# A recurrent loop on one core: side products ahead of the LSTM's, h's rest written twice, one unread product fewer per joint step

## What is computed

```python
x = x + delta_rule(lstm(x, cond), ...)      # L2_cond, L2_attn
x = x + bit_ffn(rnn(x, cond), ...)          # L2_cond2, L2_ffn

def lstm_step(h, c, xz_t):
    i, f, o, g = split(xz_t + h @ Wh)
    c = sigmoid(f) * c + sigmoid(i) * tanh(g)
    h = sigmoid(o) * tanh(c)

def delta_step(S, k, v, q, beta):           # 8 heads of 32 x 32 for each of 8 sequences
    kn = k / (norm(k) + 1e-6)
    delta = v - S @ kn
    S = tanh(beta[..., None] * S + delta[..., None] * kn[..., None, :])
    out = (S @ q) * silu(S @ q)

def rnn_step(h, xw_t):
    h = tanh(h @ Wh + xw_t)
```

## Time and profile before

| | us |
|---|---|
| median of 3 runs | 3003.81 |
| lowest and highest run | 2982.01, 3019.12 |
| the profiled execution | 3002.12 |
| its span | 3000.3 |
| busy: PE, PEld, DVE, ACT, POOL | 2498.8, 1771.7, 1727.2, 1106.1, 749.5 |

### The profile page before, as it was taken

One profiled execution on the slowest core, in us unless ns is written; L12 is line 12 of the kernel. 1 busy time (PEld: TensorE's weight loads), 2 busy tenths in 40 slices (PEclk: granted clock), 3 DMA queues, 4 the chain that ended last, 5 costly groups with the idle time before them and its releaser, 6 DMA issues. The chain is left out here.

```text
span 3000.3 us, 92538 instructions
## 1 busy us (share of the span) xinstructions
PE 2498.8 (83%) x37349; PEld 1771.7 (59%) x37354; DVE 1727.2 (58%) x7330; ACT 1106.1 (37%) x3986; POOL 749.5 (25%) x1227
## 2 busy tenths in 40 slices
PE   5998888882898889778898888889956878999998
PEld 3556666662555566555666666665533556777774
DVE  3554555556354544347776777775443865666674
ACT  1332333332133223234545555554444433333332
POOL 2210000000220000126666675766533310000000
PEclk9996555555799779899989999997856975899899
DMA  2000000001000000134645646463310000000000
GB/s 88 3 2 2 2 2 2 2 2 39 2 3 2 0 1 0 66 68 77 119 79 89 115 84 121 77 123 75 67 42 1 2 2 2 2 3 2 2 2 15
DMA packets 223769, 103.97 MB, mean 35 GB/s; under 512 B 89472, under 2 KB 220544, under 8 KB 222464
## 3 DMA queue, kind: packets, MB, share of 16 engines
q1 hardware_dynamic: 223360, 98.23, 15.9%
HBM read 89.81 MB, written 8.39 MB: 33 GB/s over the span
## 5 line engine op out<-in xcount | busy, mean ns | idle before, releaser
L649 POOL TENSOR_TENSOR l2r_beta_s<-l2r_state,l2r_beta_f 128x256 f32<-128x256 f32 x512 | 365.6, 735 | 297.7 <-ACT l2r_state L556 231.7
L556 ACT ACTIVATE l2r_state<-l2r_pre 128x256 f32<-128x256 f32 x512 | 192.7, 417 | 244.6 <-DVE l2r_pre L808 242.6
L808 DVE TENSOR_TENSOR l2r_pre<-l2r_o_ps,l2r_beta_s 128x256 f32<-128x256 f32 x512 | 194.1, 419 | 53.1 <-PE l2r_o_ps L441 32.7
L140 PE MATMUL l0r_bank<-main_x,l0r_wx_half 128*128 128x32 f32 (+2 forms) x480 | 150.1, 413 | 60.4 <-ACT l0r_out_gate L196 59.9
L140 PEld LDWEIGHTS l0r_bank<-main_x,l0r_wx_half 128*128 128x128 f32 x480 | 118.9, 311 | 81.6 <-ACT l0r_out_gate L196 79.5
L1797 PEld LDWEIGHTS l3r_bank<-main_x,l3r_wx_half 128*128 128x128 f32 x480 | 97.8, 230 | 92.6 <-issue 48.8
L441 PE MATMUL l2r_o_ps<-l2r_rows,l2r_outer 32*128 32x128 f32 x2048 | 135.1, 335 | 4.3 <-DVE l2r_rows L800 3.9
L194 ACT ACTIVATE l0r_gates<-l0r_bank 128x24 f32<-128x24 f32 x256 | 48.6, 190 | 236.3 <-PE l0r_bank L152 236.3
L1936 ACT ACTIVATE l3r_gates<-l3r_bank 128x24 f32<-128x24 f32 x256 | 48.6, 190 | 231.1 <-PE l3r_bank L1809 231.0
L228 DVE SCALAR_TENSOR_TENSOR l0r_both<-l0r_gates 128x16 f32<-128x16 f32 x256 | 45.3, 177 | 151.7 <-ACT l0r_gates L194 151.7
L152 PE MATMUL l0r_bank<-l0r_h_ring,l0r_w_part 128*128 128x8 bf16 x2304 | 102.4, 170 | 35.8 <-DVE l0r_h_ring L238 28.0
(11 more groups left out here) (590 smaller groups left out, 7324.8 us busy)
## 6 DMA issues: line engine op xcount, KB each, us to landing
l2r_beta_f<-l2r_beta_store SPq DMA_DIRECT2D x256, 256.0 KB, 7.4
main_odd_layers<-in_l SPq DMA_DIRECT2D x1, 4826.5 KB, 14.3
main_odd_layers<-in_l SPq DMA_DIRECT2D x1, 3672.0 KB, 16.2
l2r_v_store<-l2r_v_part SPq DMA_DIRECT2D x32, 96.0 KB, 3.5
l2r_v_rows<-l2r_v_store SPq DMA_DIRECT2D x16, 192.0 KB, 3.3
main_decay<-in_decay SPq DMA_DIRECT2D x1, 3072.0 KB, 10.1
main_even_layers<-in_l SPq DMA_DIRECT2D x1, 2762.5 KB, 9.6
l2r_beta_store<-l2r_beta_tok SPq DMA_DIRECT2D x64, 32.0 KB, 2.0
```

Of the source, the lines that this page charges most:

```text
L140: nc.tensor.matmul(into, wx_half[:, g * P:(g + 1) * P], x_b[:, :, w * LW + lo:w * LW + hi].rearrange("p b t -> p t b"), start=False, stop= ...
L556: nc.scalar.activation(state[:, h * 2 * P:(h + 1) * 2 * P], pre[:, h * 2 * P:(h + 1) * 2 * P], ACT.Tanh).then_inc(state_ready[h], 1)
L649: nc.gpsimd.tensor_tensor(beta_s[:, half].rearrange("p (c i) -> p c i", i=N2), state[:, half].rearrange("p (c i) -> p c i", i=N2), beta_f[ ...
L808: nc.vector.tensor_tensor(pre[:, half].rearrange("p (c n) -> p c n", c=2), o_ps[:, 2 * h:2 * h + 2, 0:P], beta_s[:, half].rearrange("p (c ...
```

## The change

Four edits, all in `recurrent_stages`:
- `UNREAD` of a joint step goes from 1 to 0; the unread product into `o_ps` stays, and so do those of the other bodies.
- TensorE's order: `lstm_pieces` (except in steps 0 and 8), `project` and `output` move from behind `lstm_products` to ahead of it, behind `spread_delta`. Their waits move with them. In steps 0 and 8 `lstm_pieces` comes ahead of the RNN's inputs.
- `split_h` has no copy any more. It writes the rest twice, into PSUM as before and with the same operands into `h_rest` in SBUF; `h_low` is the PSUM rest minus the upper half of `h_rest`, and waits for both.
- `lstm_products` reads the upper half of `h_rest` in all steps; `h_mid`, its memset and its semaphore are gone.

```diff
--- before.py
+++ after.py
@@ -255,7 +255,7 @@
 TCH = TC // 2
 SQ_STEPS = (0, 1, 2, 3, 4, 6, 7, 9)
 WIDE = 7 * B
-UNREAD = {(True, False): 2, (True, True): 1, (False, True): 3, (False, False): 0}
+UNREAD = {(True, False): 2, (True, True): 0, (False, True): 3, (False, False): 0}
 
 
 def recurrent_stages(nc, tag, x, y, wx, wh, bias, w_in, w_tok, w_q, beta_bias, w_out, sel_v, mask_r, mask_k, mask_q, mask_l, gate_sel,
@@ -271,7 +271,7 @@
         mem = Memory(nc, stack, tag)
         cand_cell, tanh_c = mem.sb("cand_cell", [P, 2 * B]), mem.sb("tanh_c", [P, B])
         h_ring = mem.sb("h_ring", [P, SLOTS, WIDE])
-        h_rest, h_mid, h_low = mem.sb("h_rest", [P, WIDE]), mem.sb("h_mid", [P, WIDE], BF16), mem.sb("h_low", [P, WIDE], BF16)
+        h_rest, h_low = mem.sb("h_rest", [P, WIDE]), mem.sb("h_low", [P, WIDE], BF16)
         w_part = [mem.sb(f"w_part{n}", [P, 4 * P], BF16) for n in range(3)]
         w_rest = mem.sb("w_rest", [P, 4 * P])
         bias_rest, bias_part = mem.sb("bias_rest", [P, 4]), mem.sb("bias_part", [P, 3, 4], BF16)
@@ -306,7 +306,7 @@
         y_b, x_b = y.rearrange("p (b t) -> p b t", t=T), x.rearrange("p (b t) -> p b t", t=T)
         x_by_half = x.rearrange("p (h b t) -> p h t b", h=2, t=T)
         names = ("consts_ready", "w_split", "bias_split", "bias_psum", "bias_ready", "xw_psum", "gates_psum", "gates_ready", "mul_ready",
-                 "cell_ready", "tanh_ready", "h_ready", "rest_ready", "h_psum", "rest_psum", "mid_h_ready", "low_ready", "xin_psum", "xp_sig_ready", "xp_ready",
+                 "cell_ready", "tanh_ready", "h_ready", "rest_ready", "h_psum", "rest_psum", "low_ready", "xin_psum", "xp_sig_ready", "xp_ready",
                  "k_psum", "v_psum", "beta_psum", "q_psum", "kv_ready", "beta_in", "q_ready", "k_sq_ready", "ssq_ready", "root_ready", "norm_ready", "inv_ready",
                  "kn_ready", "kn_stored", "kn_loaded", "v_stored", "beta_done", "beta_stored", "top_ready", "v_rested", "mid_ready",
                  "v_split", "v_loaded", "knt_psum", "knt_ready", "kn_spread", "q_spread", "outer_ready", "d_psum", "row_ready",
@@ -381,7 +381,7 @@
                     alone = n <= IN_BANK
                     if not alone:
                         pe.wait_ge(s["low_ready"], n + 1)
-                    h_parts = high(h_ring[:, (n - 1) % SLOTS, :]), high(h_rest[:, :]) if alone else h_mid[:, :], h_low[:, :]
+                    h_parts = high(h_ring[:, (n - 1) % SLOTS, :]), high(h_rest[:, :]), h_low[:, :]
                     for m in range(3):
                         if alone:
                             pe.wait_ge(s[("h_ready", "rest_ready", "low_ready")[m]], n + 1)
@@ -518,22 +518,24 @@
                         if delta is not None:
                             unread(o_ps[:, 0, :])
                             spread_delta(n)
+                        if lstm is not None and step % TCH:
+                            lstm_pieces(lstm, step, rnn)
+                        if proj is not None:
+                            project(proj, step)
+                        if out is not None:
+                            output(out, step)
                         if lstm is not None:
                             if rnn is not None and step in (0, TCH):
                                 pe.wait_ge(s["r_ready"], rnn * TC + step + 2)
                             lstm_products(lstm * TC + step)
                         if step % TCH == 0 and has_bias(k, int(step == 0)):
                             lstm_bias(*((k, 1) if step == 0 else (k + 1, 0)))
+                        if lstm is not None and step % TCH == 0:
+                            lstm_pieces(lstm, step, rnn)
                         if rnn is not None and step == 0:
                             rnn_inputs(rnn, 1, TCH + 1)
                         if rnn is not None and step == TCH:
                             rnn_inputs(rnn, TCH + 1, TC)
-                        if lstm is not None:
-                            lstm_pieces(lstm, step, rnn)
-                        if proj is not None:
-                            project(proj, step)
-                        if out is not None:
-                            output(out, step)
                         for _ in range(UNREAD[lstm is not None, delta is not None]):
                             unread(d_ps)
                         if delta is not None and n + 1 < T:
@@ -739,7 +741,6 @@
                 nc.gpsimd.tensor_tensor(w_part[2][:, :], w_rest[:, :], w_part[1][:, :], ALU.subtract).then_inc(s["w_split"], 1)
                 nc.gpsimd.memset(h_ring[:, :, B:WIDE], 0.0)
                 nc.gpsimd.memset(h_rest[:, B:WIDE], 0.0)
-                nc.gpsimd.memset(h_mid[:, B:WIDE], 0.0)
                 nc.gpsimd.memset(h_low[:, B:WIDE], 0.0)
                 nc.gpsimd.memset(kn_rows[:, :, :], 0.0)
                 nc.gpsimd.memset(v_rows[:, :, :, :], 0.0)
@@ -788,10 +789,11 @@
                     dve.wait_ge(s["h_psum"], count)
                     nc.vector.tensor_tensor(rest, lstm_at(n, 3, 4), high(h_ring[:, n % SLOTS, 0:B]),
                                             ALU.subtract).then_inc(s["rest_psum"], 1)
+                    nc.vector.tensor_tensor(h_rest[:, 0:B], lstm_at(n, 3, 4), high(h_ring[:, n % SLOTS, 0:B]),
+                                            ALU.subtract).then_inc(s["rest_ready"], 1)
                     dve.wait_ge(s["rest_psum"], count)
-                    nc.vector.tensor_copy(h_mid[:, 0:B], high(rest)).then_inc(s["mid_h_ready"], 1)
-                    dve.wait_ge(s["mid_h_ready"], count)
-                    nc.vector.tensor_tensor(h_low[:, 0:B], rest, h_mid[:, 0:B], ALU.subtract).then_inc(s["low_ready"], 1)
+                    dve.wait_ge(s["rest_ready"], n + 2)
+                    nc.vector.tensor_tensor(h_low[:, 0:B], rest, high(h_rest[:, 0:B]), ALU.subtract).then_inc(s["low_ready"], 1)
 
                 def masked(n):
                     dve.wait_ge(s["d_psum"], n + 1)
```

## The result

The changed kernel takes 3036.29 us in the median of 20 runs (2996.06 to 3066.97); the kernel before, beside it, 2998.40 in the median of 20 (2982.01 to 3021.66). So the change makes the kernel slower, by 1.3% between the medians. The ratio is only 1.0062, 95% interval [1.0034, 1.0091], because it leaves out 8 of the changed kernel's 20 runs, those over 1.5% above its fastest, and here it is the lower clock that makes runs long. Forecast were 2992 and 2958 to 3035: the median lies just above the range. The profiled execution took 3043.68 (span 3041.9, against 3000.3), with a mean granted clock of 0.791 against 0.818.

A forecast was written before the change was run, and what follows sets the result against it. It took the VectorE and ScalarE loop to bound light joint steps and beta's DMA to bound body starts. 3002.1 - 22.6 gained + 10.5 lost to the clock = 2990.0; the median, 1.7 above the profiled execution, 2992, range 2958 to 3035.

The forecast's parts named there:

- Loop (a): VectorE and ScalarE loop of a light joint step, through state, gates and h: from 2.93 to 2.80 us.
- light steps at 2.80: Joint steps with few side products on TensorE were to take 2.80 us each, as most steps would.
- h's rest: `split_h` on VectorE without the copy, L789 to the last subtraction: gain 0.12 us a step, 0.05 to 0.15.
- The unread product and the order: TensorE: 224 unread products of 0.26 us go, and side products of up to 0.55 us become free.
- loop (b): TensorE's loop in a joint step, 2.92 us: falls to 2.54 or less and no longer bounds.
- The late tanh: RNN's tanh holds `lstm_pieces`, now ahead of the LSTM's products: step 4 takes 3.22 us, step 12 2.97, step 13 3.29.
- From step 1 to beta's end 23.7: Joint body's stretch from step 1 to beta's end: 25.0 to 23.7 us, gain 14 x 1.0 = 14.4.
- Beta's chain: Beta's store and loads on SyncE until GpSimd's first product, 22.5 us a body: bounds each case, unshortened by faster steps.
- the 7.5: Gain between beta's end and the next body's step 1: 25.9 to 25.3 us, 12 x 0.6 = 7.5.
- The clock: Granted clock falls in 7 joint bodies at 3.5 us, 24.5 where 14 are lost today: 10.5 us more.
- body 13 of the kernel before: Its first step, 5.03 us with TensorE busy 4.27, kept clock 1.00: taken to show such a wait is tolerated.
- a fall in every body: Rival: the granted clock falls in all 14 joint bodies, 50 us more lost, 3031 us; chance 0.18.

The follow-up runs named there:

- e8: Changed kernel with one semaphore wait instead of two ahead of the last subtraction of h's rest; 3069.6 us, 1.0199 of the kernel before.
- e1: Changed kernel with the unread product of each joint step put back; 3000.4 us, 1.0019 of the kernel before.
- e10: Changed kernel with unread product back, beta loaded behind k, one wait before the last subtraction, `lstm_pieces` behind the LSTM's products in steps 4 and 13; 3083.6 us, 1.0285.
- e16: Changed kernel with v's store issued on SyncE behind k's store, ahead of k's load; 2981.3 us, 0.9868 of the kernel before.
- e11: Changed kernel with eight unread products at the end of step 0 of each joint body, none in its other steps; 2992.0 us, 0.9969 of the kernel before.
- e19: Kernel before with only v's store issued on SyncE behind k's store, ahead of k's load; 2956.4 us, 0.9829 of the kernel before.
- e5: Changed kernel with beta's first loads issued right behind k's, ahead of v's store and load; 3123.6 us, 1.0375 of the kernel before.

## Why the prediction failed, step by step

**Loop (a), light steps at 2.80: wrong, the term h's rest.** It gave 0.07 (0.41 to 0.34) instead of 0.12. I priced one wake-up of 0.03 between the second write and the last subtraction; there are two waits, which cost 0.10. e8, with one, shows 0.27 and steps of 2.78, 0.02 under the forecast step. Of the 0.08 by which the step is too long, 0.05 are this, and the rest is L810, which starts 0.11 after L796 instead of 0.08.

**The unread product and the order off loop (b): right.** e1 keeps 2.88 with the product, e10 2.79.

**The late tanh: right.** In body 10 step 4 took 3.24 (forecast 3.22), step 5 3.08 (3.00), step 12 2.96 (2.97), step 13 3.29 (3.29). Step 8 was 3.44 instead of 3.15 and step 15 3.16 instead of 2.80: both missed, and so the loop needs 20.7 from beta's end to step 0 where I had 19.9.

**From step 1 to beta's end 23.7: too low.** At full clock 24.3, so 0.7 gained a body where 1.3 had been the difference and 1.0 was counted: 10 us instead of 14.4.

**Beta's chain bounds every body: right but for body 6; its gain: wrong.** The first steps of bodies 3 to 15 took 5.2 on average (forecast 5.3), from 7.08 down to 3.73 in body 6, which is what they take without the wait (e16, body 4). From beta's store to GpSimd it is 22.9 a body (22.5 before), as it takes no notice of the steps; the stretch to the next step 1 stayed at 25.9 and the 7.5 did not come. The chain itself took 0.4 more and the steps behind it some 0.15; the wait went up as forecast in sign, from 57.7 to 72.5, not to 80.

**The clock: the step that failed.** Forecast were 7 falls at 3.5, 24.5 in all. The fourteen stretches from step 1 to beta's end took 389.0; 14 x 24.3 = 340.2 would be theirs at full clock, so 48.8 were lost, in 11 bodies, 4.4 each. That is the term that was mis-sized, by half, in this stretch alone. I had taken body 13 of the kernel before, which waited 2.2 us and did not fall, as the pattern for the others. It was one case, with the product in its steps: of the bodies with a wait between 2 and 3 us 3 of 10 fell with the product and 10 of 13 without. The forecast moved the bodies into that column and took the product away at the same time. It named both and put seven falls against four, but no row stood behind the seven, and none for what the missing product does. It also read the four falls of the kernel before as four waits at a body's start; body 7's came behind the stop in step 1 shown above. The rule of the Trainium skill that I set beside it (TensorE: Matmul & The Clock Gate, "What's actually happening": activity releases the throttle) spoke for more falls, and there were more. A risk in every step, as I drew from it, is not what came: in the changed kernel all 11 began in step 0 or 1 of a body, behind a wait; the missing product made them likelier and longer.

**What the forecast left out.** Bodies 16 and 17, which no edit touches: 18.0 of the 41.6 us between the two profiles. In the fourteen profiles without the edit on SyncE body 17 held its clock in two, the kernel before (43 us) and e11; in the others, those of the old kernel with one edit among them, it took 60 to 64. So the one profile of the kernel before was a lucky one in body 17, and how often that body falls in the unchanged old kernel was not counted. But the medians of 20 runs lie 37.9 apart, nearly as far as the two profiles (41.6): where the cost lies can be chance, its size is not.

**In sum.** 22.6 gained and 10.5 lost to the clock were forecast. At full clock the changed joint stretch gains about 10, and the clock takes some three times that back. The rival "a fall in every body" (3031) was close in mechanism. That it was close in time too is in part luck: it had 22.6 gained where 10 were, and 50 more lost to the clock in the joint bodies, where some 30 were lost there and 18 in bodies 16 and 17.

## What to carry over

Where the granted clock falls behind a standstill, as TensorE's did here, work that nobody reads can be cover, and time taken out of a loop that waits for a DMA becomes a longer wait and a lower clock; so first find what the loop waits for. Here it waited for the order of issues on SyncE: a load queued straight behind its own store holds up the whole queue until the store has landed, and interleaving two such pairs brought 1.7% on the kernel before (e19), with no product added or removed. And before a single body is taken as a pattern for a rare event, look at as many profiles as there are.

## What the hardware showed

- A busy TensorE did not get its clock back: in e5, body 12, it was busy for 71.43 of 71.83 us at 0.50, that is 1.2 GHz, and the body before it ran at 0.50 too; in e8 the same body took 71.84. In the changed kernel's joint stretch the half clock lasted 7 to 31 us at a time. The Trainium skill (TensorE: Matmul & The Clock Gate, "What's actually happening") says that activity releases the throttle; that row speaks against reading the profile's busy time as this activity. What else decides is open.
- Two waits one behind the other ahead of a VectorE instruction cost 0.10 us from the end of the last write (changed kernel, L796), one wait 0.03 (e8, L795).
- Two issues of a DMA that follow four of 256 KB each on the same queue took 4.5 to 6.3 us in e5 and 1.5 to 2.7 in the changed kernel.
- TensorE can stop for 1.70 us in the middle of a row of products with no releaser (e16, body 5); in all 22 such stops of over 1 us it went on 2.6 to 3.2 us after the start of a 16 KB packet of instructions.
